# A three-layer graph network on one core: edge terms made eight groups ahead and kept in SBUF, and the window sums of four groups in one PSUM bank

## The chip, the cores and the metric

One core of one Trainium2 chip. The metric is the device time of one execution in microseconds (us). TensorE is called PE, VectorE DVE, ScalarE ACT, GpSimd POOL and SyncE SP, as in the profile; L372 is line 372 of the kernel before.

## The reference

There are 12500 nodes of 128 numbers and 212500 directed edges with 16 attributes each, sorted by their target node.

```python
h = jnp.maximum(_layernorm(x, axis=-1), 0.0)
# inside the network, N = 12500 nodes:
h = h @ enc_w + enc_b
h_list = [h]
for l in range(3):
    e = edge_attr @ edge_w[l] + edge_b[l]
    msg = relu(h_list[l][src] + e)
    agg = segment_sum(msg, dst, num_segments=n_nodes)
    z = (1.0 + eps[l]) * h_list[l] + agg
    z = relu(z @ mlp_w1[l] + mlp_b1[l]) @ mlp_w2[l] + mlp_b2[l]
    h_list.append(relu(z))
out = x + concatenate(h_list, axis=1) @ out_w + out_b
```

## The kernel before

**Tiles and groups.** The edges lie in 1661 tiles of 128, four tiles to a group: 416 groups a layer, 1248 in all, the last group of each layer with one tile. The target nodes of a group lie in a window of 64 columns of `agg_t`, the transposed sum over all nodes, which stays in SBUF. A body is 16 groups. PE, ACT, DVE and SP run it as a loop (26 bodies a layer, the last written out); POOL's program is straight-line code.

**One group.** POOL fetches the source rows with four indirect gathers, one a tile (L372), into one of the 16 slots of the ring `rows`. PE multiplies the group's attributes by the edge weights into one of three PSUM banks (L620, `e_terms`, counted by `e_done`). DVE compares the targets with a row of numbers, which gives the 0/1 matrix of the window (L865, `one_hot`), and adds the edge terms, read from PSUM, to the gathered rows (L879, counted by `summed`). ACT applies the ReLU in place (L543, `relued`). PE multiplies rows and 0/1 matrix into one of two PSUM banks (L624, `sums`, counted by `agg_done`), and DVE adds the 64 columns to `agg_t` (L875, `accumulate`, `added`). In fp32 each product of a tile is two matmuls in the trace: 2 for the edge terms of a group and 8 for its sums.

**The order.** Each engine works in the order of its program. PE issues `e_terms(k + 2)` and then `sums(k)`. DVE issues `one_hot(k)`, `accumulate(k - 2)` and `add_terms(k)`: the addition of a group stands behind the sums of the group two before it.

```python
one_hot(k % NHOT, iota_ps, b * RING + k, tiles)
if k >= 2:
    accumulate(k - 2)
dve.wait_ge(e_done, first_group + (k + 1 + S0))
dve.wait_ge(gathered[k], (b + (l * uses_of_slot(k) + 1)) * (16 * TG))
add_terms(k, e_ps[k % NE_PS], tiles).then_inc(summed, 1)
```

POOL may fill the slot of group g when `agg_done` tells that the sums of group g - 16 are done:

```python
if l or group >= RING:
    g.wait_ge(agg_done, l * NG + group + 1 + S0 - RING)
```

**Nodes.** When a unit of 512 nodes has got all its edges, its two dense layers, its output term and the rows of the next layer run between groups of the edge loop (PE L643 to L664, ACT L506 and L515, DVE L916 to L922); ACT issues the store of the rows to the node table in HBM (L521). The next layer's gathers wait for the last store. SP loads the attributes of eight groups at a time into one of two buffers (L318), and writes the output after its last load.

**Prologue.** PE, ACT and DVE normalise the nodes and make the first node table. Then 25 units run through `h0_turned`, `o0` (PE L590, L598), the seeds of `agg_t` on ACT (L475, L480) and two additions on DVE (L857, L860), while POOL gathers the first 16 groups. The edge loop begins when the 25 units are done.

Of the kernel before, what the change touches and what calls it, by code (L numbers as in the profile page):

```python
# [4 lines left out]
P = 128  # L5
D = 128
KE = 16
WIN = 64
TG = 4
EP = P  # L10
# [8 lines left out]
NE_PS = 3  # L19
NA_PS = 2  # L20
NHOT = 4
# [4 lines left out]
def gnn_kernel(nc, x_t, src_t, dst_t, dst_g, ea_t, enc_w, enc_b, edge_w, edge_b, w1, b1, w2, b2,  # L26
# [18 lines left out]
    NBU = NG // HB  # L45
    L = w1.shape[0]
    HC = w1.shape[2] // D
# [13 lines left out]
    with ctx:  # L61
# [14 lines left out]
        far_idx = sb("far_idx", [P, TG], i32)  # L76
        onehot = sb("onehot", [P, NHOT, TG, WIN])
# [17 lines left out]
        iota_i = sb("iota_i", [P, WIN], i32)  # L95
# [35 lines left out]
        base_all = hot_flat[:, 0:NGP].bitcast(i32)  # L131
        stats = hot_flat[:, NGP:NGP + 6 * NT].rearrange("p (t s) -> p t s", s=6)

        bank = [ctx.enter_context(nc.psum_tensor(f"bank{i}", [P, 512], f32)) for i in range(8)]
        e_ps = bank[0:NE_PS]
        agg_ps = bank[NE_PS:NE_PS + NA_PS]
        iota_ps = bank[5][:, 0:WIN]
        zh_ps, zt_ps = bank[6], bank[7]
        turn_ps, enc_ps, h_ps = bank[0:2], bank[2:4], bank[4:6]
        o0_ps = [bank[i] for i in (6, 7, 0, 1)]  # L140
        outb_ps = bank[4]
# [52 lines left out]
        e_done = sem("e_done")  # L194
        summed = sem("summed")
        relued = sem("relued")
# [81 lines left out]
        def _(sp):  # L278
            for i in range(NI):
# [8 lines left out]
                if i == 18:  # L288
                    sp.wait_ge(s_zeroed, 3)
# [12 lines left out]
                if i == 16:  # L302
                    sp.dma_start(eps1[:, 0:L], eps.partition_broadcast(P)).then_inc(s_par, 16)
                    sp.dma_start(outw[:, :, :], out_w.rearrange("(l k) n -> k l n", k=D)).then_inc(s_par, 16)
                    sp.dma_start(outb[:, :], out_b.partition_broadcast(P)).then_inc(s_par, 16)
            sp.dma_start(dst_n, dst_g.rearrange("c (g e) -> c g e", g=GR)).then_inc(s_dst, 16)
            sp.dma_start(dst_i, dst_t).then_inc(s_dst_t, 16)
            sp.dma_start(idx[0:EP, EARLY:], src_t[:, EARLY:]).then_inc(idx_late, 16)

            for l in range(L):  # L310
                def far_pass():
                    with sp.Fori(0, NG) as g:
                        take(sp, f_next, 1)
                        sp.dma_start(far_idx[0:EP, :], src_t[:, bass.ds(g * TG, TG)]).then_inc(f_idx, 16)
                        sp.dma_start(attr[0][0:KA - 1, 0:EP], ea_t[:, bass.ds(g * EP, EP)]).then_inc(f_attr, 16)

                def load_attr(body, half):
                    sp.dma_start(attr[half][0:KA - 1, :], ea_t[:, bass.ds((body * 2 + half) * (HB * EP), HB * EP)])\  # L318
                      .then_inc(attr_in[half], 16)

                sp.wait_ge(e_done, l * NG + S0)
                load_attr(0, 0)
                load_attr(0, 1)
                with nc.Fori(1, NFULL, engines=(mybir.EngineType.SP,), hint_back_edge=True) as c:
# [3 lines left out]
                for half in range(-(-REST // HB)):  # L328
                    sp.wait_ge(e_done, NFULL * RING + l * NG + half * HB + S0 - HB)
                    load_attr(NFULL, half)  # L330
                far_passes(sp, load_extra(sp), far_pass)
            with sp.Fori(0, ND) as i:
                sp.wait_ge(o_added, i + ((L - 1) * NU + 1 + N0))
                sp.dma_start(out[:, bass.ds(i * (UT * D), UT * D)].rearrange("p (t d) -> p t d", d=D),
                             out_acc[:, bass.ds(i * UT, UT), :]).then_inc(s_out, 16)
            sp.wait_ge(o_added, L * NU + N0)
            sp.dma_start(out[:, ND * UT * D:NR * D].rearrange("p (t d) -> p t d", d=D), out_acc[:, ND * UT:NR, :])\
              .then_inc(s_out, 16)
            sp.wait_ge(s_out, 16 * NU)

        @block.gpsimd
        def _(g):
            g.sem_inc(stored, 16)
            g.memset(ident[:, :], 0.0).then_inc(s_const, 1)
            g.iota(iota_i[:, :], pattern=[[1, WIN]], base=0, channel_multiplier=0).then_inc(s_const, 1)
# [11 lines left out]
            for i in range(2):  # L357
                g.memset(attr[i][:, :], 1.0).then_inc(s_zeroed, 1)

# [16 lines left out]
            for l in range(L):  # L376
# [3 lines left out]
                def far_pass():  # L380
                    with g.Fori(0, NG):
                        take(g, f_idx, 16)
                        for j in range(TG):
                            gather(l, rows[0:EP, 0, j, :], far_idx[0:EP, j:j + 1]).then_inc(f_rows, 16)
# [4 lines left out]
                for group in range(NG):  # L389
# [7 lines left out]
                    if l or group >= RING:  # L397
# [623 lines left out]
```

## Time and profile before

| | us |
|---|---|
| median of 3 runs (lowest to highest) | 7461.86 (7454.96 to 7464.24) |
| the profiled execution's own time | 7395.73 |
| its span, first to last instruction | 7393.9 |
| busy: PE matmul / DVE / ACT / POOL | 4774.5 / 1663.8 / 999.7 / 4751.3 |
| gathers: first begins / last ends, layer 0 | 58.0 / 2472.9 |
| the same, layer 1 | 2535.6 / 4913.2 |
| the same, layer 2 | 4970.2 / 7340.6 |
| granted TensorE clock, mean | 0.558 |

The profile shows one execution. A row of the timeline has start, duration, engine, line, operation, what is written and read, and in brackets the engine's idle time before it with what ended it. "remote" stands for a release that the profile cannot name. The end of a matmul is modelled by the profiler and not observed, so when a product was really finished is read from those who waited for its semaphore.

### The profile page before, as it was taken

The numbers are of one execution on the slowest core, as the hardware profiler recorded it, in microseconds if no ns is written. First come the engines' busy times: TensorE is split into PE (matmuls) and PEld (weight loads), VectorE is DVE, ScalarE is ACT, GpSimd is POOL, SyncE is SP. The second block draws the span as 40 slices with busy tenths as digits, with TensorE's granted clock in tenths as the row PEclk, the third lists the DMA queues.
The fourth block names the chain that finished last, engine by engine and source line by source line (L and its number), as shares of the span: only waits on it lengthen the run. The fifth ranks groups of instructions, "written<-read, shape, count | busy, mean of one in ns | idle before, by whom it ended". The sixth has DMA issues, their size and how long they took to land.

```text
span 7393.9 us, 56283 instructions
## 1 busy us (share of the span) xinstructions
PE 4774.5 (65%) x14396; PEld 3131.3 (42%) x14397; DVE 1663.8 (23%) x4168; ACT 999.7 (14%) x1597; POOL 4751.3 (64%) x5075
## 2 busy tenths in 40 slices
PE   5666666666666646666666666673666666666667
PEld 4444444444444424444444444442444444444444
DVE  4222222222222212222222222221222222222222
ACT  4111111111111101111111111110111111111111
POOL 5666666666666466666666666646666666666664
PEclk7555555555555555555555555555555555555555
DMA  3122212222222112222222222211111111111112
GB/s 116 53 54 54 55 53 54 54 55 54 54 54 54 44 49 54 55 55 54 54 55 55 53 54 56 55 43 51 51 51 52 51 52 51 52 51 51 52 52 72
DMA packets 191126, 404.82 MB, mean 55 GB/s; under 512 B 85159, under 2 KB 87927, under 8 KB 190439
## 3 DMA queue, kind: packets, MB, share of 16 engines
q0 software_dynamic: 159456, 326.88, 17.0%
q1 hardware_dynamic: 21759, 56.75, 2.6%
q10 hardware_dynamic: 9840, 20.48, 0.8%
q14 instruction: 55, 0.45, 0.0%
q8 instruction: 16, 0.26, 0.0%
HBM read 378.08 MB, written 25.69 MB: 55 GB/s over the span
## 4 chain that ended last, share of the span: by engine, by line
another core or an unknown queue 44%; PE 27%; issue 18%; DVE 6%; DVEq 3%; ACT 3%; POOL 0%; DMA 0%; ACTq 0%
PE bank L624 14%; PE bank L620 9%; DVE rows L879 3%; ACT rows L543 2%; DVE onehot L865 2%; PE bank L651 1%; PE bank L664 1%; PE bank L643 1%; DVEq L939 1%; DVE agg_t L875 1%; PE bank L645 1%; DVEq L247 1%; DVEq L875 0%; PE bank L661 0%
## 5 line engine op out<-in xcount | busy, mean ns | idle before, releaser
L372 POOL DMA_INDIRECT rows<-h_table,idx x4983 | 4714.0, 946 | 2575.5 <-issue 1417.7
L624 PEld LDWEIGHTS bank<-onehot,rows 128*128 128x128 f32 x9966 | 2178.6, 310 | 3367.3 <-ACT rows L543 1966.2
L624 PE MATMUL bank<-onehot,rows 128*128 128x64 f32 x9966 | 2158.1, 394 | 2162.8 <-ACT rows L543 1599.7
L620 PE MATMUL bank<-edgew,attr 65*128 65x512 f32 x2496 | 2279.0, 1026 | 9.6 <-DMA w2s<-w 9.6
L543 ACT ACTIVATE rows<-rows 128x512 f32<-128x512 f32 x1248 | 783.1, 628 | 5381.1 <-DVE rows L879 4213.0
L875 DVE TENSOR_TENSOR agg_t<-bank,agg_t 128x64 f32 x1248 | 278.1, 223 | 4790.4 <-remote 3542.9
L879 DVE TENSOR_TENSOR rows<-bank,rows 128x512 f32<-128x512 f32 x1248 | 857.6, 687 | 83.2 <-DMA rows<-h_table,idx 35.2
L620 PEld LDWEIGHTS bank<-edgew,attr 65*128 65x128 f32 x2496 | 677.7, 316 | 280.6 <-issue 280.6
L865 DVE TENSOR_TENSOR onehot<-bank,dst_rel 128x256 f32<-128x256 f32 x1248 | 518.3, 415 | 205.4 <-issue 205.4
L651 PE MATMUL bank<-hid,w2s 128*128 128x512 f32 x300 | 195.3, 769 | 192.5 <-ACT hid L506 124.8
L664 PE MATMUL bank<-outw,h_t 128*128 128x128 f32 x588 | 151.7, 423 | 62.0 <-ACT h_t L515 58.5
L506 ACT ACTIVATE hid<-bank,b1s 128x512 f32<-128x512 f32 (+1 forms) x150 | 101.0, 678 | 539.1 <-remote 297.3
L664 PEld LDWEIGHTS bank<-outw,h_t 128*128 128x128 f32 x588 | 142.5, 326 | 64.2 <-ACT h_t L515 60.4
L651 PEld LDWEIGHTS bank<-hid,w2s 128*128 128x128 f32 x300 | 59.8, 233 | 256.5 <-ACT hid L506 155.7
L643 PE MATMUL bank<-agg_t,w1s 128*128 (+1 forms) x150 | 149.1, 1097 | 1.7 <-DVE agg_t L875 1.7
L645 PE MATMUL bank<-agg_t,w1s 128*128 (+1 forms) x150 | 124.5, 928 | 0.0
L661 PE MATMUL bank<-ident,h_t 128*128 128x128 f32 x196 | 45.6, 372 | 107.2 <-ACT h_t L515 100.7
L916 DVE COPY h_n<-bank 128x512 f32<-128x512 f32 (+1 forms) x50 | 34.1, 681 | 356.3 <-remote 242.8
L515 ACT ACTIVATE h_t<-bank,b2s 128x512 f32<-128x512 f32 (+1 forms) x75 | 50.9, 678 | 369.1 <-remote 232.3
L922 DVE TENSOR_TENSOR out_acc<-bank,out_acc 128x512 f32 (+1 forms) x75 | 50.6, 674 | 199.3 <-remote 101.8
L645 PEld LDWEIGHTS bank<-agg_t,w1s 128*128 128x128 f32 x150 | 50.3, 335 | 74.9 <-issue 74.4
L661 PEld LDWEIGHTS bank<-ident,h_t 128*128 128x128 f32 x196 | 33.7, 224 | 112.1 <-ACT h_t L515 104.8
(83 smaller groups left out, 478.6 us busy)
## 6 DMA issues: line engine op xcount, KB each, us to landing
rows<-h_table,idx POOLq DMA_INDIRECT x4983
attr<-ea_t SPq DMA_DIRECT2D x156, 256.0 KB
h_table<-h_n ACTq DMA_DIRECT2D x48, 256.0 KB
h_table<-rows SPq DMA_DIRECT2D x24, 256.0 KB, 2.1
out<-out_acc SPq DMA_DIRECT2D x24, 256.0 KB
out_acc<-x_t ACTq DMA_DIRECT2D x4, 1280.0 KB, 11.5
rows<-dst_g SPq DMA_DIRECT2D x1, 832.0 KB
rows<-dst_t SPq DMA_DIRECT2D x1, 832.0 KB
```

Of the source, the lines that this page charges most:

```text
L372: return g.indirect_dma_start(dst, None, h_table[l % 2], bass.IndirectOffsetOnAxis(ap=index, axis=0))
L506: nc.scalar.activation(hid[:, c, 0:cols], ps[:, 0:cols], ACT.Relu, bias=b1s[:, l * HC + c:l * HC + c + 1])\
L543: nc.scalar.activation(part, part, ACT.Relu).then_inc(relued, 1)
L620: return nc.tensor.matmul(dst[0:EP, 0:tiles * D], cols, edgew[:, l, 0:tiles * D], start=True, stop=True)
L624: last = nc.tensor.matmul(dst[:, 0:WIN], rows[0:EP, slot, j, :], onehot[0:EP, hot_slot, j, :], start=(j == 0), stop=(j == tiles - 1))
L643: nc.tensor.matmul(zh_ps[:, 0:cols], w1s[:, 0:D], moving, start=True, stop=True).then_inc(z_done, 1)
L645: nc.tensor.matmul(zt_ps[:, 0:cols], w1s[:, D:2 * D], moving, start=True, stop=True).then_inc(z_done, 1)
L651: last = nc.tensor.matmul(zh_ps[:, 0:cols], w2s[:, c, :], hid[:, c, 0:cols], start=(c == 0), stop=(c == HC - 1))
L664: last = nc.tensor.matmul(zh_ps[:, j * D:(j + 1) * D], cols[:, j, :], outw[:, l + 1, :], start=True, stop=True)
L865: return v.tensor_tensor(onehot[0:EP, slot, 0:tiles, :], numbers[0:EP, :].unsqueeze(1).broadcast_to([EP, tiles, WIN]), dst_rel[0:EP, bass. ...
L875: return v.tensor_tensor(cols, ps[:, 0:WIN], cols, ALU.add)
L879: return v.tensor_tensor(part, ps[0:EP, 0:tiles * D].rearrange("p (t d) -> p t d", d=D), part, ALU.add)
```

## The change

- `e_terms` runs eight groups ahead of `sums` (before: two), into four banks (before: three), and across the ends of bodies and layers. ACT copies each group's edge terms from PSUM into a ring of eight in SBUF (`keep_terms`, counted by `placed`), five groups ahead of its ReLU. DVE adds them from SBUF.
- The first eight `e_terms` and five copies are issued within the 25 units of the prologue, from unit 8 on.
- The sums of four groups (a batch) fill 256 columns of one bank, and `agg_done` rises once a batch. DVE makes the 0/1 matrices of a batch together, and accumulates a batch after the additions of the next batch's first three groups. POOL waits once a batch.
- The stores of the next node table move from ACT to SP, between SP's attribute loads; in the last layer the output is written there too. Far passes, which this input does not need, get a buffer of their own.
- In the prologue `o0` has two banks (before: four) and the output bias is added from SBUF, not from a PSUM bank. Node steps on PE move from the second to fourth group of a half body to the third, fifth and seventh; on ACT from the third and fourth to the fourth and sixth.

```diff
-NE_PS = 3
+NE_PS = 4
 NA_PS = 2
-NHOT = 4
+AHEAD = 8
+KEPT = 5
+NTERM = 8
+BATCH = 4
+NHOT = 2 * BATCH
...
-                    if l or group >= RING:
-                        g.wait_ge(agg_done, l * NG + group + 1 + S0 - RING)
+                    if (l or group >= RING) and group % BATCH == 0:
+                        g.wait_ge(agg_done, l * NQ + (group - RING) // BATCH + 1 + S0)
...
+            def keep_terms(l, b, k):
+                tiles = real_tiles(b, k)
+                act.wait_ge(e_done, b * RING + (l * NG + k + 1 + S0))
+                nc.scalar.copy(terms[0:EP, k % NTERM, 0:tiles, :],
+                               e_ps[k % NE_PS][0:EP, 0:tiles * D].rearrange("p (t d) -> p t d", d=D))\
+                  .then_inc(placed, 1)
...
                         nc.scalar.activation(part, part, ACT.Relu).then_inc(relued, 1)
+                        if k + KEPT < RING:
+                            keep_terms(l, b, k + KEPT)
+                        elif not isinstance(b, int):
+                            keep_terms(l, b + 1, k + KEPT - RING)
...
                 o0(i)
+                if i == HB:
+                    pe.wait_ge(edge_bias, 1)
+                if HB <= i < HB + AHEAD:
+                    e_terms(0, 0, i - HB)
...
+                def sums(b, k):
+                    batch, i = k // BATCH, k % BATCH
+                    if i == 0:
+                        pe.wait_ge(hot_made, b * (RING // BATCH) + (l * NQ + batch + 1 + S0))
+                    pe.wait_ge(relued, b * RING + (l * NG + k + 1))
+                    last = window_sums(agg_ps[batch % NA_PS][:, i * WIN:(i + 1) * WIN], k, k % NHOT, real_tiles(b, k))
+                    if i == BATCH - 1:
+                        last.then_inc(agg_done, 1)
...
+                def add_group(b, k):
+                    tiles = real_tiles(b, k)
+                    dve.wait_ge(placed, b * RING + (l * NG + k + 1 + S0))
+                    dve.wait_ge(gathered[k], (b + (l * uses_of_slot(k) + 1)) * (16 * TG))
+                    part = rows[0:EP, k, 0:tiles, :]
+                    v.tensor_tensor(part, terms[0:EP, k % NTERM, 0:tiles, :], part, ALU.add).then_inc(summed, 1)
...
+                        for batch in range(2 * half, 2 * half + 2):
+                            later, then = (b, batch + 1) if batch < 3 else (b + 1, 0)
+                            add_groups(later, then, 0, 3)
+                            accumulate(b, batch)
+                            if batch < 2:
+                                one_hots(b, batch + 2)
+                            else:
+                                one_hots(b + 1, batch - 2)
+                            add_groups(later, then, 3, 1)
```

## Rows read from the trace of the kernel before

**Rows 1.** The page's chain that ended last, by engine.
```profile
another core or an unknown queue 44%; PE 27%; issue 18%; DVE 6%; DVEq 3%; ACT 3%; POOL 0%; DMA 0%; ACTq 0%
```

**Rows 2.** The windows of the gather stretches and between: length, busy and count by engine.
```profile
58.00:2472.90 2414.90, 1544.67 (x4712) 1013.27 (x4712) 565.59 (x1365) 338.52 (x520) 1571.70 (x1661) 0.57 0.21 55
2472.90:2535.60 62.70, 55.13 (x182) 38.37 (x182) 20.42 (x53) 12.89 (x22) 0.03 (x1) 0.61 0.07 18
2535.60:4913.20 2377.60, 1502.89 (x4466) 979.76 (x4466) 514.43 (x1272) 294.57 (x470) 1571.31 (x1661) 0.55 0.20 54
4913.20:4970.20 57.00, 52.36 (x182) 36.78 (x182) 19.59 (x52) 13.00 (x22) 0.02 (x1) 0.65 0.08 20
4970.20:7340.60 2370.40, 1530.04 (x4383) 992.64 (x4384) 491.02 (x1228) 295.39 (x471) 1570.98 (x1661) 0.54 0.20 52
7340.60:7393.90 53.30, 48.76 (x168) 33.79 (x166) 16.61 (x45) 11.75 (x20) 0.00 (x0) 0.66 0.26 93
```

**Rows 3.** The waits: who waited for whom, us in total, times, longest.
```profile
POOL rows L372 <- remote: 903.0, 305, 10.6
POOL rows L372 <- PE bank L624: 107.5, 59, 30.7
DVE agg_t L875 <- remote: 3542.9, 410, 27.0
```

**Rows 4.** The page's group of the gathers: busy, mean ns, idle before.
```profile
L372 POOL DMA_INDIRECT rows<-h_table,idx x4983 | 4714.0, 946 | 2575.5 <-issue 1417.7
```

**Rows 5.** The timeline inside layer 1, PE, POOL and DVE around one wait.
```profile
3954.97 1.81 PE L624 MATMUL bank<-onehot,rows 128*128 128x64 f32 x8
...
3960.02 2.02 PE L620 MATMUL bank<-edgew,attr 65*128 65x512 f32 x2
...
3966.87 0.95 POOL L372 DMA_INDIRECT rows<-h_table,idx  x1 [0.30 <-issue]
...
3971.37 0.22 DVE L875 TENSOR_TENSOR agg_t<-bank,agg_t 128x64 f32 x1 [13.50 <-remote]
3971.51 0.94 POOL L372 DMA_INDIRECT rows<-h_table,idx  x1 [3.70 <-remote]
```

**Rows 6.** The timeline at the start of layer 1, PE, DVE and POOL.
```profile
2573.05 1.97 PE L624 MATMUL bank<-onehot,rows 128*128 128x64 f32 x8 [10.89 <-issue]
...
2599.47 0.23 DVE L875 TENSOR_TENSOR agg_t<-bank,agg_t 128x64 f32 x1 [26.80 <-issue]
...
2601.06 1.97 PE L624 MATMUL bank<-onehot,rows 128*128 128x64 f32 x8 [24.22 <-ACT rows L543]
...
2650.78 0.95 POOL L372 DMA_INDIRECT rows<-h_table,idx  x1 [10.43 <-remote]
```

**Rows 7.** The timeline after the last gather of layer 0.
```profile
2481.30 1.81 PE L624 MATMUL bank<-onehot,rows 128*128 128x64 f32 x8
...
2484.71 1.81 PE L624 MATMUL bank<-onehot,rows 128*128 128x64 f32 x8
...
2486.66 0.23 DVE L875 TENSOR_TENSOR agg_t<-bank,agg_t 128x64 f32 x1 [2.26 <-PE bank L624]
```

**Rows 8.** The timeline where the edge loop begins, POOL and PE.
```profile
189.05 0.95 POOL L372 DMA_INDIRECT rows<-h_table,idx  x1 [30.71 <-PE bank L624]
...
196.71 1.81 PE L624 MATMUL bank<-onehot,rows 128*128 128x64 f32 x8
```

**Rows 9.** The timeline of a gather beside a DVE instruction from SBUF to SBUF.
```profile
3237.40 0.94 POOL L372 DMA_INDIRECT rows<-h_table,idx  x1 [0.30 <-issue]
...
3238.49 0.48 DVE L918 TENSOR_SCALAR agg_t<-h_t,eps 128x512 f32 x1
3238.65 1.13 POOL L372 DMA_INDIRECT rows<-h_table,idx  x1 [0.30 <-issue]
```

**Rows 10.** Groups of ACT and DVE by shape: busy, mean ns, idle before.
```profile
L441 ACT COPY rows<-bank 128x512 f32<-128x512 f32 x14 | 8.1, 579 | 0.4 <-PE bank L583 0.3
...
L879 DVE TENSOR_TENSOR rows<-bank,rows 128x512 f32<-128x512 f32 x1245 | 856.7, 688 | 83.2 <-DMA rows<-h_table,idx 35.2 <-remote 27.7 <-issue 14.8
```

More of the change, by code:

```diff
@@ L194, in gnn_kernel @@
         e_done = sem("e_done")
+        placed = sem("placed")
         summed = sem("summed")
+        hot_made = sem("hot_made")
         relued = sem("relued")
@@ L327, in _ @@
                         load_attr(c, half)
[L328 to L335, printed above, removed]
+                        store_unit(c * 2 + (half - 2))
+                for half in range(2):
+                    if l < L - 1:
+                        sp.wait_ge(e_done, NFULL * RING + l * NG + half * HB + HB + S0)
+                        load_attr(0, half)
+                    store_unit(NFULL * 2 + half)
+                first = load_left(sp)
+                far_passes(sp, n_far, far_pass)
+                nodes_left(sp, first, store)
+                if l < L - 1:
+                    sp.wait_ge(rows_ready, ND + l * NU + (1 + N0))
+                    sp.dma_start(h_last[(l + 1) % 2], h_n[:, 0:LAST, :].rearrange("p t d -> p (t d)"))\
+                      .then_inc(stored, 16)
             sp.wait_ge(o_added, L * NU + N0)
@@ L689, in edge_body @@
-                    for k in range(min(2, groups)):
-                        e_terms(k)
-                    for k in range(groups):
-                        half, kk = k // HB, k % HB
-                        if kk == 0 and groups - k >= HB:
-                            unit = load_unit(pe, b * 2 + half)
-                        if k + 2 < groups:
-                            e_terms(k + 2)
-                        sums(k)
-                        if kk in (1, 2, 3) and groups - half * HB >= HB:
+                            unit = load_unit(pe, b * 2 + half)
@@ L903, in _ @@
             dve.wait_ge(o0_added, NI)
-            own(v.tensor_copy(iota_ps, iota[:, :]))
             dve.wait_ge(seeded0, NI)
+            for ps in iota_ps:
+                own(v.tensor_copy(ps, iota[:, :]))
             n_far = load_extra(dve)
@@ new lines, in add_groups, with accumulate @@
+                def add_groups(b, batch, first, count):
+                    for k in range(batch * BATCH + first, batch * BATCH + first + count):
+                        add_group(b, k)
+                def accumulate(b, batch):
+                    at = [dve.snap(bases[k], min_val=0, max_val=NP)
+                          for k in range(batch * BATCH, (batch + 1) * BATCH)]
+                    dve.wait_ge(agg_done, b * (RING // BATCH) + (l * NQ + batch + 1 + S0))
+                    for base, k in zip(at, range(batch * BATCH, (batch + 1) * BATCH)):
+                        dve.wait_ge(added, b * RING + (l * NG + k + S0))
+                        i = k % BATCH
+                        add_window(base, agg_ps[batch % NA_PS][:, i * WIN:(i + 1) * WIN]).then_inc(added, 1)
@@ new lines, in _ @@
+                for half in range(2):
+                    load_bases(NFULL, half)
+                    for batch in range(2 * half, 2 * half + 2):
+                        if batch < 3:
+                            add_groups(NFULL, batch + 1, 0, 3)
+                        if batch == 3:
+                            take_unit(NFULL * 2 + 1)
+                        accumulate(NFULL, batch)
+                        if batch < 2:
+                            one_hots(NFULL, batch + 2)
+                        elif batch == 2 and l < L - 1:
+                            one_hots(0, 0)
+                        if batch < 3:
+                            add_groups(NFULL, batch + 1, 3, 1)
+                        if batch == 0:
+                            take_unit(NFULL * 2)
```

210 lines of the change are left out of this document (109 added, 101 removed).

## The prediction

> **What bounds the kernel now.** The windows first. The gathers fill three stretches of 2414.9, 2377.6 and 2370.4 us; what lies between and behind them is 62.7, 57.0 and 53.3 us [rows 2]. So the question is what paces POOL. One gather takes 0.946 us and is followed by 0.30 us of issue [rows 4, 5], a period of 1.25 us. The 1661 gathers of a layer would take 2076 us back to back; the stretches are longer by 339, 301 and 294 us, 934 in all. The waits say where that goes: POOL waited 305 times for "remote" and 59 times for the window sums L624, 1010.5 us together [rows 3]. Without the 0.30 us of issue that stands before every gather (364 x 0.30 = 109) that is 901 us. Both are `agg_done`, the only semaphore that gather waits for here: the ring of 16 groups is full. POOL is never short of room because it is slow; it is held by the groups behind it.
>
> Why are those slow? The chain ends in 44% "another core or an unknown queue" [rows 1], and the longest wait of all is DVE's accumulation behind "remote", 3542.9 us in 410 waits [rows 3]. The timeline names it. The sums of a group were issued at 3954.97 and modelled to end at 3956.8, PE's last work after them at 3962.0; DVE, which waits for that signal, went on at 3971.37, and POOL at 3971.51, 3.7 us after its last gather had ended [rows 5]. **PE's completion signals come late while POOL gathers.** After the last gather of a layer they are on time: sums that end at 2486.5 release DVE at 2486.66, and one group's sums follow the other's after 3.41 us (2481.30 to 2484.71), less than POOL's 5.0 [rows 7]. At the start of a layer, where 84 gathers follow each other without a pause, they are latest: sums issued at 2573.05, the next at 2601.06 [rows 6]. So lateness comes with gathering and ends soon after POOL pauses. Because DVE adds group k only behind the sums of k - 2, just two groups can be in work behind a late signal, and every pause of POOL frees little: 364 pauses for 1248 groups, one per 3.4 groups, 2.8 us each.
>
> The Trainium skill ("Perfetto Trace Analysis", Tensor Engine Instruction) says the profiler's end of a matmul is an estimate, and that the semaphore goes out only when PSUM has acknowledged the writes. The rows agree that the modelled end isn't the signal: 14.6 us lie between them in [rows 5].
>
> **The change, part by part.**
> 1. *Waits of POOL.* After the change seven groups can be in work behind a missing signal: the batch of four whose `agg_done` is awaited and the next three, which DVE has added before it accumulates. The edge terms run eight ahead, so they are not what lacks. When POOL pauses, the signals of all of them come out, `agg_done` of one batch at once and the next one group later; that lets POOL fill two batches, 8 groups or 40 us, to the next pause. I take one pause per two batches: 1248 / 8 = 156. Length: 3.7 us after a short run of gathers [rows 5], 10.43 us after 84 in a row, 105 us [rows 6]; scaled by the run, 10.43 x 40 / 105 = 4.0. I take 3.8, so 156 x (3.8 - 0.3) = 546 us. Before it was 901, of which 30.4 is the prologue's full ring [rows 8]; 871 remain. Saved: **-325 us**. Bounds: no pause at all, -871; one at each of the 312 batch waits, 312 x 3.5 = 1092, that is +221.
> 2. *Start.* POOL resumed at 189.05, with the first group's sums [rows 8]. Now it needs four: the fourth ended at 198.5 (196.71 + 1.81), less three edge terms of 1.7 us (half of 3.41) that no longer stand between, 193.5. The eight products of 1.7 us moved into the units, two `o0` banks for four, and bias additions from SBUF cost DVE and PE at most some us in a stretch where POOL waits 30 us anyhow, but they delay the first sums. **+10 us** (bounds +5 and +25).
> 3. *Ends of layers.* 14 groups of 3.41 us follow the last gather now (47.7 us, [rows 2, 7]). A batch-wise ring stands on average some 10 groups behind: 4 x 3.41 x 3 = **-40 us**. Bounds: 0, and -90 if the chain is caught up.
> 4. *DVE's addition* has both inputs in SBUF. Its own time stays 0.69 us [rows 10]. But a gather that began inside the SBUF-to-SBUF L918 took 1.13 us instead of 0.94 [rows 9], 0.19 more. An addition of 0.69 covers the start of a gather in 0.69 / 1.25 = 55% of cases; with a mean delay of half the 0.19, 1248 x 0.55 x 0.095 = **+65 us**. Bounds: 0 (the mean of all gathers is 946 ns [rows 4], with today's additions beside them), and 1248 x 0.19 = 237.
> 5. *ACT's copies*: 1248 x 0.579 [rows 10] = 723 us, on an engine busy 1000 of 7394 us. Hidden by its wait for DVE. They stand in order before the next ReLU: if the edge terms five ahead aren't signalled, the ReLU waits too. They were issued three groups earlier than the copy, 15 us at POOL's pace, as late as the signal in [rows 5] and less than in [rows 6]; that is why I don't take a caught-up chain. No cost of its own.
> 6. *SP* now waits for the store's rows between attribute loads; a half is asked for eight groups (40 us) before use. The stores leave ACT. Nothing. The 0/1 matrices and accumulations are as many as before.
>
> The Trainium skill ("SBUF — State Buffer", Who interferes with whom) has a rule against part 4: a DVE instruction with two SBUF inputs contends with a GpSimd instruction that reads SBUF, and the later one is blocked until the other is through. By it every addition that a gather meets could cost up to the whole 0.69 us, not 0.19. [rows 9] agree in kind, with 0.19 us in place of the 0.32 that were left of L918.
>
> Sum, against the profiled execution's 7395.7: -325 + 10 - 40 + 65 = -290, 7106. The median of the runs is 7461.9, 0.9% above that execution, so 7106 x 1.009 = **7169 us** for the median.
>
> **The rivals.**
> - *A, POOL-bound.* The lateness stays under the slack of 15 us and POOL pauses only in the prologue: -871 + 10 - 90 + 65 gives 6510, median 6568. For it: the new order tolerates 14.6 us. Against: 26.8 us in [rows 6], under just the uninterrupted gathering that this case needs. 15%. A case between (a pause per three to four batches, 6750 to 7000) gets 13%.
> - *B, the pause is a debt.* POOL must stand still for the same share of time however the work is queued, since 10.4 us of pause follow 105 us of gathering. Then parts 2 to 4 remain, with no gain at the ends: +10 + 65, 7471, median 7538; without the collisions 7473. 15%. It decides if a pause per two batches is over 871 / 156 = 5.6 us net.
> - *C, a pause at every batch.* `agg_done` now comes once per four groups, so a signal that is late stops POOL at each batch: +221 + 10 + 65, with the ends unchanged, gives 7692, median 7761. It decides if the seven groups in work don't reach over two batches. For it: four sums must all be signalled before anything is freed. Against: on each pause all signals so far came together [rows 5]. 12%.
> - *My forecast*: 45%, own range 7030 to 7330.
>
> **How the numbers follow.** No change that this kernel's measurement can tell is about 0.2%, 15 us. Faster: 45 + 15 + 13, and 2 of B: 75%. Same: 5% from B. Slower: 8 from B and 12 from C, 20%. Range: from A's 6568, a little lower as A is a limit, to B's 7538: 6550 to 7540 leaves out C and a part of A.
>
> **What would show it.** In the new profile POOL's waits for `agg_done` should be some 156 of 3 to 5 us, not 364; DVE's waits on sums should be longer and rarer; gathers should be longer by 0.1 to 0.2 us where an addition meets them and their mean should rise from 946 to about 960 ns. ACT busy should rise to some 1720 us. I'm wrong if POOL's period is 1.25 us throughout (A), if its idle total is unchanged (B), if it stops once per batch (C), or if DVE waits for `placed` with ACT behind PE: then the lookahead of part 5 was too short.

## The result, and the profile after

The median of 12 runs went from 7461.0 us (7454.96 to 7468.37) to **7442.95 us** (7431.67 to 7463.78): a ratio of 0.9979, 95% interval 0.9969 to 0.9989. That is 18 us, just beyond the 15 us that the forecast called no change. The forecast was 7169.

The traces differ by more, and the other way, because the profiled execution of before lay 65 us under its median while that of after (7441.92) is at its own: spans of 7393.9 and 7440.1. The windows, in the order of [rows 2]:

```profile
57.39:2518.42 2461.03, 1579.52 (x4798) 1052.94 (x4798) 575.39 (x1391) 523.25 (x942) 1597.54 (x1661) 0.57 0.20 54
2518.42:2554.79 36.37, 32.13 (x114) 21.29 (x113) 11.86 (x35) 10.64 (x21) 0.00 (x0) 0.73 0.10 28
2554.79:4959.48 2404.69, 1499.12 (x4536) 1003.85 (x4536) 522.11 (x1288) 477.34 (x888) 1599.48 (x1661) 0.56 0.20 53
4959.48:4996.40 36.92, 32.28 (x115) 21.54 (x115) 11.87 (x35) 9.63 (x19) 0.00 (x1) 0.73 0.10 28
4996.40:7396.08 2399.68, 1516.21 (x4406) 1001.26 (x4407) 493.34 (x1230) 473.51 (x878) 1605.73 (x1661) 0.55 0.20 53
7396.08:7440.10 44.02, 34.88 (x128) 26.47 (x127) 12.25 (x35) 12.47 (x24) 0.00 (x1) 0.62 0.04 11
```

The gather stretches grew from 7162.9 to 7265.4 us together (+102.5), the ends of layers shrank from 173.0 to 117.3 (-55.7), the first gather came 0.6 earlier: +46.2, the difference of the spans. The page's chain (answers to [rows 1]), its group of the gathers ([rows 4]), and the waits ([rows 3]):

```profile
another core or an unknown queue 60%; issue 12%; DVE 11%; PE 10%; DVEq 5%; ACT 1%; POOL 1%; DMA 0%; ACTq 0%
L404 POOL DMA_INDIRECT rows<-h_table,idx x4983 | 4802.8, 964 | 2543.0 <-issue 1449.3
L496 ACT COPY terms<-bank 128x512 f32<-128x512 f32 x1248 | 719.4, 576 | 2012.9 <-remote 1404.6
```
```profile
DVE agg_t L919 <- remote: 4135.6, 249, 36.5
POOL rows L404 <- remote: 873.0, 218, 12.7
POOL rows L404 <- PE bank L670: 116.2, 10, 51.1
```

POOL pauses less often, 228 times for 364, and longer, 4.3 us for 2.8. Less 0.30 us of issue each, the pauses are 921 us in all, and without the one at the start (51.1, before 30.7) **870 us, where before had 871**. There are fewer and longer pauses, as forecast; their sum did not move. Inside layer 1, PE and POOL in the timeline around one pause:

```profile
4026.98 0.27 PE L670 MATMUL bank<-onehot,rows 128*128 128x64 f32 x1 [2.53 <-issue]
4027.33 0.94 POOL L404 DMA_INDIRECT rows<-h_table,idx  x1 [0.30 <-issue]
4028.38 0.29 PEld L670 LDWEIGHTS bank<-onehot,rows 128*128 128x128 f32 x1 [2.51 <-issue]
4028.58 0.94 POOL L404 DMA_INDIRECT rows<-h_table,idx  x1 [0.30 <-issue]
4029.78 0.27 PE L670 MATMUL bank<-onehot,rows 128*128 128x64 f32 x1 [2.53 <-issue]
...
4033.57 0.94 POOL L404 DMA_INDIRECT rows<-h_table,idx  x1 [0.30 <-issue]
...
4040.13 1.29 DVE L919 TENSOR_TENSOR agg_t<-bank,agg_t 128x64 f32 x4 [26.44 <-remote]
4040.18 0.94 POOL L404 DMA_INDIRECT rows<-h_table,idx  x1 [5.66 <-remote]
```

PE does one load or one product per 1.40 us (4026.98, 4028.38, 4029.78) while POOL gathers, and nothing that the profile shows holds it. The sums' signal reaches DVE and POOL at 4040.1, after 5.66 us of POOL's silence. The whole trace has 1009 steps of 1.37 to 1.43 us between the starts of PE's records, 1413 us together. The trace of before has 5: there the eight products of a group run in 1.81 us [rows 5], and only their signal is late. So with eight groups of work ahead PE itself was held, which queueing ahead was meant to prevent. This is read from the two traces; no run was made to test it.

### The profile page after: what moved, and what is told of

It is laid out like the page before. It is cut to its first block, busy times and chain, and to the rows that moved or that the text cites. A ratio compares the mean times of both kernels' runs of the same rounds, so it can differ in the third digit from the quotient of the medians.

```text
span 7440.1 us, 58485 instructions
## 1 busy us (share of the span) xinstructions
PE 4734.6 (64%) x14396; PEld 3163.5 (43%) x14397; DVE 1662.6 (22%) x4168; ACT 1540.3 (21%) x2845; POOL 4839.9 (65%) x5076
## 4 chain that ended last, share of the span: by engine, by line
another core or an unknown queue 60%; issue 12%; DVE 11%; PE 10%; DVEq 5%; ACT 1%; POOL 1%; DMA 0%; ACTq 0%
DVE rows L980 5%; PE bank L670 4%; PE bank L644 4%; DVE agg_t L919 3%; DVE onehot L909 2%; DVEq L978 1%; DVEq L977 1%; DVEq L987 1%; DVEq L919 1%; DVEq L996 1%; POOL rows L404 1%; DVEq L909 0%; PE bank L689 0%; ACT rows L573 0%
## 5 line engine op out<-in xcount | busy, mean ns | idle before, releaser
L404 POOL DMA_INDIRECT rows<-h_table,idx x4983 | 4802.8, 964 | 2543.0 <-issue 1449.3
L670 PEld LDWEIGHTS bank<-onehot,rows 128*128 128x128 f32 x9966 | 2234.5, 304 | 3462.7 <-issue 2870.6
L644 PE MATMUL bank<-edgew,attr 65*128 65x512 f32 x2496 | 2219.9, 979 | 314.8 <-issue 313.9
L496 ACT COPY terms<-bank 128x512 f32<-128x512 f32 x1248 | 719.4, 576 | 2012.9 <-remote 1404.6
L644 PEld LDWEIGHTS bank<-edgew,attr 65*128 65x128 f32 x2496 | 639.6, 299 | 519.3 <-issue 514.8
L980 DVE TENSOR_TENSOR rows<-terms,rows 128x512 f32<-128x512 f32 x1248 | 806.3, 689 | 189.4 <-issue 116.0
L909 DVE TENSOR_TENSOR onehot<-bank,dst_rel 128x256 f32<-128x256 f32 x1248 | 441.3, 416 | 1.0 <-DVE bank L950 1.0
L697 PE MATMUL bank<-hid,w2s 128*128 128x512 f32 x300 | 240.9, 952 | 0.0
L697 PEld LDWEIGHTS bank<-hid,w2s 128*128 128x128 f32 x300 | 82.3, 303 | 69.2 <-issue 66.6
L631 PE MATMUL bank<-outw,hid 128*128 128x128 f32 x200 | 34.4, 328 | 72.0 <-ACT hid L516 44.4
## 6 DMA issues: line engine op xcount, KB each, us to landing
out_acc<-x_t ACTq DMA_DIRECT2D x4, 1280.0 KB, 11.5
```

The source lines that it names most:

```text
L404: return g.indirect_dma_start(dst, None, h_table[l % 2], bass.IndirectOffsetOnAxis(ap=index, axis=0))
L496: nc.scalar.copy(terms[0:EP, k % NTERM, 0:tiles, :], e_ps[k % NE_PS][0:EP, 0:tiles * D].rearrange("p (t d) -> p t d", d=D))\
L644: return nc.tensor.matmul(dst[0:EP, 0:tiles * D], cols, edgew[:, l, 0:tiles * D], start=True, stop=True)
L670: last = nc.tensor.matmul(dst, rows[0:EP, slot, j, :], onehot[0:EP, hot_slot, j, :], start=(j == 0), stop=(j == tiles - 1))
L697: last = nc.tensor.matmul(zh_ps[:, 0:cols], w2s[:, c, :], hid[:, c, 0:cols], start=(c == 0), stop=(c == HC - 1))
L909: return v.tensor_tensor(onehot[0:EP, slot, 0:tiles, :], numbers[0:EP, :].unsqueeze(1).broadcast_to([EP, tiles, WIN]), dst_rel[0:EP, bass. ...
```

## Experiments

Each row is one or two kernels. "Before" is the kernel before, measured beside them on the same chip. "Recorded" counts the semaphore events that the trace holds. e1 to e4 and e11 to e18 are single executions.

| run | kernel | us | before | recorded |
|---|---|---|---|---|
| (first) | before, profiled | 7395.7 | | 24,121 |
| (first) | after, profiled | 7441.9 | 7461.0 | 21,003 |
| e1 | before, sums of 1 tile of 4 | 6319.9 | 6321.5 | 92,584 |
| e2 | before, edge terms as 4 products | 6323.2 | 6321.5 | 92,537 |
| e3 | before, gathers of 32 rows | 5939.8 | 6321.5 | 92,564 |
| e4 | before, addition from SBUF | 6349.7 | 6321.5 | 92,569 |
| e5 | before | 6331.6 | 6332.0 | 92,577 |
| e6 | after | 6369.4 | 6332.0 | 93,206 |
| e7, e8 | sums twice, before / after | 6324.5 / 6373.6 | 6322.3 | 92,489 / 93,153 |
| e9, e10 | sums three times, before / after | 6857.8 and 7022.3 / 6479.3 | 6322.7 | 92,392 / 92,874 |
| e11 | after, sums of 1 tile of 4 | 7295.2 | 7459.7 | 16,819 |
| e12 | after, gathers of 32 rows | 7443.1 | 7459.7 | 19,934 |
| e13 | after, 2 of 4 gathers | 4500.7 | 7437.4 | 20,408 |
| e14 | after, a plain load for 4 gathers | 2923.4 | 7437.4 | 33,462 |
| e15 | after, sums twice | 7753.2 | 7437.4 | 27,691 |
| e16, e17 | 3 of 4 gathers, after / before | 4823.2 / 4787.2 | 6321.1 | 73,267 / 72,610 |
| e18 | after, 3 of 4 gathers | 5643.9 | 7406.0 | 19,595 |

The first four were meant to tell what the late signals grow with.

```diff
 # e1: window sums of the first tile only      (matmuls per group 10 -> 4)
-                for j in range(tiles):
+                for j in range(1):
 # e2: edge terms as four products of 128 columns      (10 -> 16)
-                return nc.tensor.matmul(dst[0:EP, 0:tiles * D], cols, edgew[:, l, 0:tiles * D], start=True, stop=True)
+                for j in range(tiles):
+                    last = nc.tensor.matmul(dst[0:EP, j * D:(j + 1) * D], cols, edgew[:, l, j * D:(j + 1) * D],
+                                            start=True, stop=True)
 # e3: 32 rows per gather
-gather(l, rows[0:EP, slot, t % TG, :], idx[0:EP, t:t + 1])
+gather(l, rows[0:EP // 4, slot, t % TG, :], idx[0:EP // 4, t:t + 1])
 # e4: the addition's other input from a constant SBUF tile
-v.tensor_tensor(part, ps[0:EP, 0:tiles * D].rearrange("p (t d) -> p t d", d=D), part, ALU.add)
+v.tensor_tensor(part, still[0:EP, 0:tiles, :], part, ALU.add)
```

> The kernel before, whose window sums multiply only the first of four tiles: per group of 512 edges TensorE has 2 matmul records and 2 weight loads less of 128 x 64 ... 4 in all where there were 10 of each; the output leaves out three quarters of the messages. Gathers, additions and ReLUs are as before. T1 (while POOL gathers, TensorE's completions pass at a limited rate of instructions, so that POOL must stand still in proportion to them): 4 instead of 10 matmuls per group take some 60 % of the 901 us of pauses away, 6800 to 6900 us. T2 (the pauses are the price of the gathers' own traffic, whatever TensorE does): pauses stay near 900 us, 7300 to 7460. T3 (my forecast: latency between dependent groups, not a debt): TensorE's chain of a group shrinks by 1.7 us, the pauses by a third at most, 7100 to 7300.

> The kernel before, with each group's edge terms multiplied as four products of 128 columns instead of one of 512: the same columns and result, but 16 instead of 10 matmuls per group. T1: the pauses grow by 16/10, 901 to about 1440 us, total 7900 to 8000. T2: no change beyond 1 %, 7390 to 7500. T3: the chain of a group grows by a few tenths of a us, 7400 to 7550.

> The kernel before, whose gathers fetch only the first 32 of the 128 rows of a tile, as many gathers as before; the output leaves out three quarters of the messages' node terms. TensorE, VectorE and ScalarE do all they did. T2: the traffic falls to a quarter, and with it the lateness of TensorE's signals and the pauses for sums; POOL's or TensorE's own pace is left: 5000 to 6500 us. T1: if any gather instruction holds TensorE's signals, the pauses stay some 900 us and only a shorter gather shows; 6700 to 7300. T3: with shorter gathers POOL waits more, since the chain of a group is the limit: 5800 to 6800.

> The kernel before, whose addition reads a constant SBUF tile in place of the PSUM bank with the edge terms (they are still multiplied, and left out of the sum): the collision of VectorE instructions with two SBUF inputs and gathers by itself, with the old order of work. Forecast of part 4: gathers 13 ns longer on average (946 to 959), +65 us, 7500 to 7540. As in the profile of after (a gather that begins in such an addition 982 ns): 946 to 964, 60 to 100 us, unless the pauses shrink by as much, in which case 7440 to 7480 (debt of POOL: only the share of time it stands still counts).

None of them answered, and none of the expected times for T1 to T3 came (e3's 5939.8 lies inside two of them by chance), because the question was gone: the kernel before itself took 6321.5 us, 1140 less. All four lie where POOL's pace puts them: 4983 gathers at a period of 1.248 us (32 rows: 867 ns for 944, so 1.171), and no pause. e4 gives the price of the collisions alone: +28 us (spans 6347.8 and 6319.6, e5), the gathers' 4703.7 us becoming 4731.4. (The 982 ns in its expectation don't come out of the profile of after: the 626 gathers that begin inside such an addition there take 1105 ns on average.)

So the two kernels themselves were measured again, unchanged.

> The kernel before, unchanged, for a trace of it beside the runs that took 6321 us. If the pauses depend on the chip or on the state it is in, and not on the kernel: either some 6320 us with no wait of POOL for sums, as in the first four experiments, or some 7460 us with 900 us of them, as in the first profile. A time between would say that the lateness of TensorE's signals has more than two levels.

> The changed kernel, unchanged. Where the kernel before takes 6320 us there are no pauses to save; then only the start (+10), the ends of layers (-40) and the collisions are left (by the addition of the fourth experiment +28, by the gathers of the profile after, 18 ns longer, +89): 6290 to 6400 us, a ratio of 0.995 to 1.012. Where the kernel before takes 7460 us, the ratio is again 0.998.

Before 6331.6 (8 runs), after 6369.4 (4 runs): a ratio of **1.0061** (1.0044 to 1.0078). The chain and the group of the gathers of the kernel before, then the same of the changed kernel:

```profile
POOL 34%; PE 24%; DMA 17%; issue 14%; DVE 6%; ACT 5%; DVEq 0%; SPq 0%; POOLq 0%; ACTq 0%
L372 POOL DMA_INDIRECT rows<-h_table,idx x4983 | 4703.7, 944 | 1552.7 <-issue 1244.3
```
```profile
POOL 73%; issue 24%; PE 1%; DVE 1%; DMA 0%; ACT 0%; SPq 0%; POOLq 0%; DVEq 0%; ACTq 0%
L404 POOL DMA_INDIRECT rows<-h_table,idx x4983 | 4729.8, 949 | 1568.8 <-issue 1517.7
```

No "another core or an unknown queue", no wait with the name "remote" in any view, and a trace with 92,577 semaphore events in place of 24,121 for the same program. In the first profiles three quarters of these events are not recorded, and it is only there that waits are put down to "remote": the event that would name the releaser is missing. In the trace of before, 51% of TensorE's recorded signals between 2700 and 4800 us (341 of 673) come over 1.3 us after the start of the last gather, that is in a pause, though the pauses are a seventh of the time (334 us of layer 1's 2378). In e5 it is 7 of 955. The two behaviours are not bound to a chip: over all runs, signals were on time on chips 8, 5, 7, 2 and 0, and late on 7, 9 and 14. What brings the one or the other was not found.

Where they are on time, the changed kernel's extra 46 us of span (6365.7 against 6319.6) come from these places. The windows of the first stretch, kernel before and then after:

```profile
57.55:2132.71 2075.16, 1607.45 (x4870) 1007.87 (x4870) 575.07 (x1409) 347.98 (x537) 1569.28 (x1661) 0.58 0.24 64
```
```profile
57.68:2158.98 2101.30, 1627.43 (x4872) 993.56 (x4872) 601.40 (x1402) 545.75 (x956) 1584.58 (x1661) 0.59 0.24 63
```

The first stretch costs 26.1 us, the other two 5.8 and 5.3; between and behind them it is 49.5 for 40.7, +8.8. Of the 26.1, 19.7 are there when the 65th gather starts (158.95 against 139.3). The timeline of the changed kernel in the prologue, where the bias additions now read SBUF, and at the full ring:

```profile
77.88 0.94 POOL L404 DMA_INDIRECT rows<-h_table,idx  x1 [0.30 <-issue]
...
79.05 0.69 DVE L904 TENSOR_TENSOR out_acc<-outb,out_acc 128x512 f32<-128x512 f32 x1
79.12 1.43 POOL L404 DMA_INDIRECT rows<-h_table,idx  x1 [0.30 <-issue]
...
158.95 0.95 POOL L404 DMA_INDIRECT rows<-h_table,idx  x1 [11.02 <-PE bank L670]
```

A gather that starts 0.07 us into such an addition takes 1.43 us: 0.49 more, with 0.62 left of the addition. 22 gathers met one, at a mean of 1293 ns. Then the ring is full for 11.02 us until four sums are done. In the loop few gathers start inside an addition (83 of 4983, mean 1049 ns; in the late trace of after it is 626). A likely reason is that the addition follows the landing of a group's gathers at a fixed place in POOL's period; that was not tested.

The next four make TensorE short by hand, to see whether the new order could have helped against a real shortage. Each sum is multiplied once or twice more, into 64 columns that nobody reads (same result).

```diff
+                for part in (1, 0):            # e7; (2, 1, 0) in e9, and alike in e8, e10
-                for j in range(tiles):
+                    for j in range(tiles):
-                    last = nc.tensor.matmul(dst[:, 0:WIN], rows[0:EP, slot, j, :], onehot[0:EP, hot_slot, j, :],
+                        last = nc.tensor.matmul(dst[:, part * WIN:(part + 1) * WIN], rows[0:EP, slot, j, :],
+                                                onehot[0:EP, hot_slot, j, :], start=(j == 0), stop=(j == tiles - 1))
```

> The kernel before, whose window sums are multiplied twice, the first time into 64 columns of the same bank that nobody reads: the same result, 1.7 us more of TensorE per group. On a chip where its signals are on time, this makes TensorE itself short: 4817 us busy + 1248 x 1.7 = 6940 us, against 6225 us of gathers. It puts a shortage of TensorE's throughput in the place of the late signals. Expected: 6950 to 7250 us, with POOL waiting for sums some 800 us in all, in many waits of 1 to 4 us, as in the first profile. If the late signals are there too, 8000 us or more.

> The changed kernel with the same doubling. Debt (T1, my rival B: what POOL must wait is set by how much TensorE gets done in all, not by the order of the work): within 1 % of the kernel before with the doubling, POOL's waits fewer and longer with about the same sum, as 364 to 228 in the first pair of profiles. T3 (my forecast: the work eight groups ahead takes latency off POOL's path): 2 to 4 % faster than it.

Twice was not enough: e7 took 6324.5 us, not 6950 or more. TensorE's busy time went from 4816.5 to 6056.3 us, 96% of an unchanged span. So neither expectation of e8 had its case; it is 49 us behind e7, where without the doubling the changed kernel is 38 behind.

> The kernel before, whose window sums are multiplied three times, twice into 64 columns of the same bank that nobody reads (same result). The doubled sums still fitted: TensorE went from 4817 to 6056 us busy, 96 % of the span, and the granted clock from 0.576 to 0.626. One more copy adds at least the same 1240 us: 7300 us busy or more, now beyond the gathers' 6225. Expected 7350 to 7900 us, with POOL waiting for sums 1000 us or more in some 300 to 600 waits. This is a shortage of TensorE's throughput made by hand, on a chip where its signals are on time.

> The changed kernel with the same tripling. Debt (rival B): within 1 % of the kernel before with the tripling; POOL's waits fewer and longer (at most one per batch of four groups, 312), with about the same sum. T3 (my forecast, latency): 2 to 4 % faster than it.

e9 took 6857.81 and 7022.30 us (the granted clocks are 0.731 and 0.711; its trace is of the longer one and shows the kind of the difference, not its size), e10 6474.57 and 6483.95 (0.773 and 0.771). POOL's waits for sums in e9 and the window of its layer 1:

```profile
POOL rows L372 <- PE bank L625: 592.8, 372, 5.6
```
```profile
2396.00:4614.30 2218.30, 2184.83 (x10888) 1819.48 (x10889) 523.70 (x1274) 295.36 (x471) 1570.88 (x1661) 0.71 0.22 58
```
The same two of e10:

```profile
POOL rows L404 <- PE bank L671: 68.7, 8, 24.7
```
```profile
2260.50:4346.70 2086.20, 2058.09 (x11188) 1716.01 (x11188) 541.37 (x1299) 494.82 (x899) 1580.31 (x1661) 0.77 0.24 62
```

The new order takes 5.5% off the shorter run of e9, more than the 2 to 4% expected, and ends POOL's pauses. But that isn't the hidden latency that I had argued: TensorE is 98% busy in both traces, and what changed is its own pace, 6324.0 us for the same 34,328 products instead of 6865.6, at a higher granted clock. Why it is granted more in the new order was not tested. So the order of work can help where TensorE is short. That was not the case of the first profiles, where TensorE was busy for 65 and 64% of the span.

In the next runs the late signals were back (7459.7 for the kernel before). All experiments with late signals vary the changed kernel; the kernel before was only measured beside them.

> The changed kernel with window sums of only the first of four tiles: 4 instead of 10 matmuls per group; the output leaves out three quarters of the messages. If TensorE's signals are late on this chip (the kernel before then takes 7460 us): T1, pauses in proportion to its instructions, 6800 to 6900 us; T2, pauses of the gathers' own traffic, 7350 to 7450 us. If they are on time (6320 to 6333 us for the kernel before), POOL sets the time alone: 6340 to 6366 us, and what lies above the kernel before is not TensorE's.

> The changed kernel with gathers of 32 of the 128 rows; the output leaves out three quarters of the messages' node terms. If TensorE's signals are late on this chip: T2, the pauses go with the traffic, below 6300 us; T1, they stay, 6900 to 7100 us. If they are on time, POOL's gathers of 867 ns, as with the kernel before, set the time: 5940 + 46 = 5985 us.

e11 is 148 us faster for 7470 matmuls less, 0.02 us each: T1 falls, it needed some 600. (T2 allowed 7350 at the least and got 7295.) e12 is the sharper one. Its waits and its group of the gathers:

```profile
POOL rows L405 <- remote: 1164.4, 258, 16.3
POOL rows L405 <- PE bank L671: 146.4, 15, 50.9
```
```profile
L405 POOL DMA_INDIRECT rows<-h_table,idx x4983 | 4394.5, 882 | 2958.5 <-issue 1522.4
```

POOL is busy 408 us less, its waits for sums are 322 us more (1310.8 for 989.2) and its issue 73 (1522.4 for 1449.3), and the time is the same (7443.1 for a median of 7442.95). A quarter of the bytes changed nothing (T2 needed under 6300 and falls), and neither did shorter instructions. T1's number, 6900 to 7100, was missed too. What had stayed the same was the number of gathers.

```diff
 # e13 (and 3 for 2 in e16, e18, and in the old order e17); each group waits for so many
-                    tiles = min(TG, NTR - group * TG)
+                    tiles = min(2, NTR - group * TG)
 # e14
-                    for t in range(group * TG, group * TG + tiles):
-                        gather(l, rows[0:EP, slot, t % TG, :], idx[0:EP, t:t + 1]).then_inc(gathered[slot], 16)
+                    first = group % ND * UC
+                    g.dma_start(rows[0:EP, slot, :, :],
+                                h_table[l % 2][first:first + UC, :].rearrange("(p t) d -> p t d", t=TG))\
+                     .then_inc(gathered[slot], 16)
```

> The changed kernel with only two of a group's four gathers; the output leaves out half of the messages' node terms; TensorE, VectorE and ScalarE do all they did. With late signals (the kernel before 7460 us), so far 5.76 us per group whether a gather takes 964 or 882 ns (7443 us both) and 5.65 with 60 % fewer matmuls (7295). T2b, the debt is per gather instruction (1.44 us each, pause included): 2 x 1.44 = 2.9 us per group, so TensorE's own 3.4 to 4 us set the time, 5000 to 5400 us. T4, a rate of TensorE's side that does not know the gathers: again 5.7 us per group, 7400 us. With signals on time (6322 to 6332 for the kernel before) there is no such question: 5000 to 5400 us.

> The changed kernel whose four indirect gathers of a group are one plain load of 512 consecutive rows, still issued by POOL; the output leaves out the choice of rows. Same bytes. T2b: the lateness goes with the indirect gathers, 4950 to 5400 us, TensorE the bound. T4: 7000 to 7400 us, if TensorE is slow by itself.

> The changed kernel with every window sum multiplied twice (6373 us where the signals were on time). With late signals: T1, a debt by TensorE's instructions, 18 instead of 10 matmuls per group, 8000 us or more; T2b and T4, by the slope of one tile to four (147 us for 6 matmuls per group) 7440 + 200 = 7640 us at most.

T4 falls with e13 and e14: without half of the gathers, or with none, TensorE does the same work in 4500.7 and 2923.4 us. Both lie below what T2b said (5000 and 4950 at the least): 3.6 and 2.3 us per group, at granted clocks of 0.646 and 0.935, for 0.568 in the changed kernel. The chains say that it then sets the time itself, wholly in e14 and mostly in e13 (e13, then e14):

```profile
PE 80%; another core or an unknown queue 8%; issue 6%; DVE 4%; ACT 1%; DVEq 1%; DMA 0%; ACTq 0%; POOL 0%
```
```profile
PE 96%; DVE 2%; DMA 1%; ACT 1%; issue 0%; SPq 0%; DVEq 0%; ACTq 0%
```

e15 took 7753.2 us, 310 more for 9966 matmuls more, 0.03 each. That is above the 7640 of T2b and below the 8000 of T1; TensorE is 86% busy there and 68% of the chain, so a part of it is TensorE's own time. What is left is T2b, 1.43 us for each gather whatever it does on POOL, and it gives a number for three gathers per group.

> The changed kernel with three of a group's four gathers, 3738 in all; the output leaves out a quarter of the messages' node terms. With late signals, a line through the runs so far: 1.43 us per gather, whatever its own time on POOL, and 0.02 us per matmul. 7443 - 1245 x 1.43 = 5660 us. If the debt were one of time (a share of POOL's busy time) or of TensorE, it would be 4983 to 3738 gathers at POOL's period of 1.25 us, 7443 - 1556 = 5890 us or more. With signals on time: 3738 x 1.248 and the ends, or TensorE's 4500 to 4800, so 4700 to 4900 us.

> The kernel before with three of four gathers. With late signals: the price of 1.43 us per gather is the same in the old order, 7460 - 1780 = 5680 us, within 1 % of the changed kernel. With signals on time TensorE is near its limit, as with the tripled sums, where the new order gained 5.5 %: 4850 to 5100 us, 2 to 5 % above the changed kernel.

> The changed kernel with three of four gathers once more, for a run where the signals are late (with them on time it took 4823 us). Late: 1.43 us per gather, 5660 us. A debt in time at POOL's period of 1.25 us: 5890 us or more. TensorE's own 4500 to 4830 us if three gathers per group leave it room. On time: 4823 us again, and the question stays open.

e16 and e17 met signals on time (4823.2 and 4787.2: 1245 gathers less at 1.242 us each, and the changed kernel again 36 us behind, not ahead as I expected of e17). The old order with three gathers was never measured with late signals. e18 met late ones and took **5643.9 us, where T2b said 5660** and a debt in POOL's time 5890 or more. The waits of e18:

```profile
POOL rows L405 <- remote: 611.3, 210, 9.3
POOL rows L405 <- PE bank L671: 120.4, 18, 46.5
```

With late signals a gather costs (7442.95 - 5643.92) / 1245 = **1.445 us**, on time (6369.44 - 4823.2) / 1245 = 1.242 us, POOL's own period. The first compares two chips: the kernel before took 7406.0 us beside e18, 55 us under its 7461.0. If the changed kernel is as much faster there, the price is 1.40 us. The traces give it without that doubt. The windows of layer 1 in e12 and e18:

```profile
2561.34:4959.10 2397.76, 1514.02 (x4501) 1007.80 (x4502) 509.52 (x1277) 474.48 (x880) 1461.43 (x1661) 0.56 0.08 20
```
```profile
1961.02:3758.96 1797.94, 1428.64 (x4508) 965.58 (x4509) 516.03 (x1276) 474.07 (x880) 1210.88 (x1246) 0.59 0.22 56
```

Per gather that is 1.444 and 1.443 us, and 1.448 in the changed kernel (2404.69 / 1661), though the gathers themselves take 882, 973 and 964 ns.

A second reading is near this one: a limit on semaphore events, since a gather ends in 16 of them. Take each program's count from its complete trace (or, for e13 and others not run on time, the same less 16 per gather left out) and divide by the span: before 12.5 events per us, after 12.5, e11 12.8, e12 12.5, e13 11.9, e15 12.0, e18 13.0. On time the same programs reach 14.6, e16 15.2 and e3 15.6. e14 needs only 11.5, and its trace is the one late trace that holds all of them; but e13 needs only 11.9 and holds 20,408 of some 53,370. At the 12.5 of the changed kernel e18 would have taken 73,286 / 12.53 = 5850 us, where the price per gather said 5660 and 5643.9 were measured. So the late runs follow the number of gathers more closely than the number of events. One run on another chip doesn't separate the two for good, as each gather brings its 16.

Why TensorE is held while POOL gathers stays open. The Trainium skill ("NOTIFIC — the notification-queue block", Overflow: three behaviours, one of which stalls the engine) says that the block that writes event records can be set so that a full ring stalls the engine that produces them. The traces fit that in part only: TensorE is held, but 24,121 of 92,577 events are recorded, and the same section has discarded records as another setting than the stall. No run shows the ring itself. Every timed execution here comes with its core's span and clock, so it was recorded too, and what either kernel takes without recording was not measured.

## Why the prediction was wrong

- **Diagnosis.** That POOL's pauses wait for late signals of TensorE was right, as far as the traces name them. I took the lateness as a delay that a longer queue can cover, though the line named no releaser because the trace had lost it. The 1.44 us per gather could be read from the trace of before, and it was the real pace. Two windows of 64 of its periods each, in layer 1, with PE, PEld, DVE, ACT and POOL:

```profile
3943.10:4035.00 91.90, 58.83 (x180) 38.30 (x180) 20.83 (x53) 11.91 (x19) 60.56 (x65) 0.57 0.20 54
4035.00:4127.00 92.00, 59.24 (x180) 38.47 (x180) 20.92 (x53) 11.91 (x19) 60.68 (x65) 0.57 0.21 54
```

- **Part 1, waits of POOL (-325): the step that failed.** "One pause per two batches", 156 of 3.8 us: measured 228 of 4.3, and the sum 870 us for 871. The number of pauses fell, and each grew by as much. A pause was not the price of a dependency; it paid the difference between POOL's period of 1.25 us and 1.44. e12 shows this in its pure form: POOL's shorter work came back as waits, and the time stayed. Rival B had it ("the pause is a debt"), at 15%, and its sign, an unchanged idle total, is what came. Its picture of [rows 6], 10.4 us of pause after 105 us of gathers, should have weighed more than the 3.7 us of [rows 5].
- **Part 2, start (+10, bounds 5 and 25).** POOL resumed at 212.57 for 189.05, +23.5 with late signals, inside the bounds; +19.7 on time. The sum gave the bias additions some us of DVE's and PE's time and didn't see that, with two SBUF inputs, they would stretch gathers: on time they stretched 22 by 7.7 us in all, and the four sums at the full ring were waited for 11.02 us. With late signals the wait at the full ring grew from 30.7 to 51.1 us.
- **Part 3, ends of layers (-40).** -55.7 with late signals, the right sign and size: 36.4, 36.9 and 44.0 us for 62.7, 57.0 and 53.3. On time there is no chain to shorten (15.5, 12.6, 12.7 us), and it costs 8.8.
- **Part 4, collisions (+65, bounds 0 and 237).** The gathers' busy time rose by 88.8 us (4714.0 to 4802.8). 626 of them started inside an addition, 50% of the additions for 55% forecast, at a mean of 1105 ns for 944. So the mis-sized term is the mean delay, 0.16 us for 0.095. On time the busy time rose by 26.1 (e6) or 27.7 (e4). The delay follows what is left of the addition, less some 0.13 us: with 0.6 to 0.69 us left 0.49 on average (121 gathers), with 0.3 to 0.4 left 0.21 (69), with under 0.1 left nothing (146). The 0.32 left and 0.19 lost of [rows 9] lie on the same line, so 0.19 was not the most that a collision can cost. The rule of the Trainium skill ("SBUF — State Buffer", Who interferes with whom), blocked until the other is through, is thus close, but for those 0.13 us.
- **What the collisions cost with late signals** stays open. In the two traces the 88.8 us stand in the time: the gather stretches grew by 102.5, that is by these 88.8 and by 20.4 of waiting at the first full ring, less 6.7 elsewhere. But the trace of before is 65 us under its median. Were these 65 us spread over the 4983 gathers, the kernel before would need 1.444 and 1.440 us per gather in layers 1 and 2, the changed one 1.448 and 1.445. By that estimate, as by e12, the pauses would take up most of it. On time the collisions are most of what the loop loses.
- **The total.** The traces differ by +46.2 us, B's parts gave +75 and mine -290. Both sums were then scaled by 1.009, because the profiled execution of before lay under its median; that of after did not (7441.92 for a median of 7442.95). That is 67 of the 95 us by which B's 7538 missed the 7443 measured.
- **Part 5, ACT's copies hidden.** Right: 719.4 us for 723, and DVE waited 7.2 us in all for them by name, with late signals. **Part 6, SP**, nothing seen.
- The median of 7442.95 is inside the range (6550 to 7540), at its slow end, by the width of the range and not by the mechanism. The gain is 0.2% for 3.9% forecast, and where signals are on time the changed kernel is slower by 0.6%. None of the full kernels here beats both: on time, the kernel before has no pause left, and 6219 of its 6320 us are 4983 periods of POOL.

## What to carry to other kernels

A wait whose releaser the profile cannot name may be a sign that records are missing, as here; run the unchanged kernel again, at another time and on another chip, before building on it. Ask of each stall whether it is a delay or a rate: shorten the work of the engine that waits, and if the waits grow by the same amount (e12), it is a rate, and queueing ahead did not help here. And where instructions of a nearly fixed cost pace a kernel, here 4983 gathers at 1.25 us each, fewer of them pay (e16, e17), and smaller ones pay little: on time, a quarter of the rows saved 6% (e3).

## What was not expected of the hardware

- The kernel before on the chip numbered 7 took 6320.7 to 6334.4 us (9 runs) and nine minutes later 7459.7 (one run).
- A gather of 32 rows takes 867 ns, of 128 rows 944 (e3, e5): by these two, an estimate of 0.8 ns per row on a base of about 0.84 us.
- TensorE's granted clock is 0.576 in e5, 0.626 in e7, 0.711 and 0.773 in e9 and e10, and 0.935 in e14, where it did e6's work in 2850 us of busy time for 4921. These are means over the two levels, 1.2 and 2.4 GHz. So the 4800 us of busy TensorE in the page of before were no measure of what it needs. The slices of e14:

```profile
PE   5799999999999989999999999998999999999999
PEclk9858999999999965999999999997599999999999
```
